# The first loads of a gated cross-attention and mixture-of-experts kernel on two DMA queues, with idle matmuls ahead of the first real one

## The chip, the cores and the metric

The kernel runs on one core of one Trainium2 chip. The metric is the device time of that core in microseconds (us), lower is better. The kernel before takes 236.41 us, the median of 3 runs (236.2 to 236.48).

## What is computed

Cut to what matters, for x of 8 x 256 x 256 and a context of 8 x 120 x 256 (float32):

```
q = layernorm(x) @ Wq + bq;  k = ctx @ Wk + bk;  v = ctx @ Wv + bv
x = x + tanh(g_xattn) * softmax(q @ k.T) * 256**-0.5 @ v      # per batch item
h = layernorm(x)
e = argmax(h @ router_w.T)                                    # one of 8 experts
x = x + tanh(g_ffn) * (silu(h @ gate_w[e].T) * (h @ up_w[e].T)) @ down_w[e].T
```

## The kernel before, in words

The kernel is written by hand, engine by engine, with semaphores. Each engine works through its own list in order, so an instruction that waits holds back all that stands behind it on that engine. The rows of x are 2,048 tokens, held as 16 tiles of 128 in `xin`, two tiles for each of the 8 batch items.

**First stage, around which the change lies.** The queries and keys are never built. One 256 x 256 matrix `MT` is made from the query and key weights, and its product with the context is `A`, so that the scores are the normalised x times `A`.

- SP issues the loads of `wkT` (L299), `wqT` (L300), the context `ctx_sb` (L301, in the buffer `both`), then the eight pieces of x (L306) with `wv` (L305) ahead of the third piece, then the first raw expert weights (L313, L324, L326).
- ACT issues, on its own DMA queue, the two gates (L517, L518: 4 bytes copied to each of 128 partitions), the value bias `bvb` (L519) and the router weights `wrT` (L520). It then waits for both gates (`d_g`, L521) and takes their tanh (L522). Only then does it come to the eviction of `MT` (L527 to L531), in two halves `m`, each behind TensorE's `t_mt`.
- TensorE waits for both weights (`d_wq`, L690), makes `MT` in PSUM (L693), then a small product with the bias (L699). It waits for the context (L703) and for both evicted halves of `MT` (`a_mt`, L704), makes `A` in four parts (L708), waits for `bvb` and `wrT` (`d_sm`, L713), runs L715, and then, once ACT has evicted `A` (L579), turns the normalised x of item 0 (L724), makes its values (L733) and its scores (L744).
- DVE subtracts on the weights (L951, L953), then takes the statistics of x items 0 and 1 as they land (L958, L962), their scales (L944 to L948) and their normalisation (L939). It waits for the tanh (L968) and for `d_sm` (L970), takes the statistics of the other six items (L958, L962), waits for TensorE's L715 (L972) and L733 (L979), and comes to `minima(0)` (L985), which needs the scores of item 0. Behind that stand the scales of the other items and the normalisation of item 2.
- POOL makes constants (L358 to L378).

**Attention loop.** For each of the 8 items the engines pass a tile round: TensorE transposes and multiplies, ACT takes exponentials, DVE minima, residuals and statistics. ACT also splits the first three experts' weights into high and low parts between items (`split_first`, L583), and POOL makes the low parts (L409, L413) as soon as ACT's high part is there.

**Routing and experts.** Tokens are sorted by expert, then up to 23 tiles of 128 tokens are gathered, multiplied with their expert's weights (L876, L888) and scattered. Before each of two waits in the routing, TensorE runs useless bf16 matmuls (`spin`, L822).

The lines in question:

```
pe.wait_ge(d_wq, 32)                       # L690, then L693, L699
pe.wait_ge(d_ctx, 16)                      # L703
pe.wait_ge(a_mt, C)                        # L704, then L708
act.wait_ge(d_g, 32)                       # L521
act.activation(tg[:], gates[:], ACT.Tanh)  # L522, then L526: act.wait_ge(t_mt, m + 1)
```

Of the kernel before, what the change touches and what calls it, by code (L numbers as in the profile page):

```python
# [26 lines left out]
BF16 = mybir.dt.bfloat16  # L27
# [6 lines left out]
P = 128  # L34
B, S, H = 8, 256, 256
# [3 lines left out]
C = H // P  # L39
# [21 lines left out]
def flamingo_moe(nc, x, ctxT, g_x, g_f, WqT, WkT, Wv, bv, WrT, Wgu, Wd, WdL, out):  # L61
    with ExitStack() as stack:
        def sb(name, shape, dt=F32):
            return stack.enter_context(nc.sbuf_tensor(name, shape, dt))

        def sem(name):
            return stack.enter_context(nc.semaphore(name))
# [7 lines left out]
        ctx_sb = both[:, 0:C * B * K].rearrange("p (c n) -> p c n", c=C)  # L75
# [5 lines left out]
        wqT = sb("wqT", [P, C, H + 1])  # L81
# [37 lines left out]
        x1 = sb("x1", [P, 2, TB, H])  # L119
# [2 lines left out]
        rs2 = sb("rs2", [P, 2, NTOK])  # L122
        x1T = wkT[:, :, 0:H]
        wqx = xnT
        pick = sb("pick", [P, NTOK])
        oh = sb("oh", [P, NTOK + 1, E], BF16)

# [15 lines left out]
        def part(room, start, *dims):  # L143

            size = 1
            for d in dims:
                size *= d
            names = " ".join("abc"[:len(dims)])
            view = room[:, start:start + size]
            if len(dims) > 1:  # L150
                view = view.rearrange(f"p ({names}) -> p {names}", **dict(zip("abc", dims)))
            return view, start + size
# [3 lines left out]
        ohlo, _ = part(free_c[:, at:at + NTOK * P // 2].bitcast(BF16), 0, NTOK, P)  # L156
        at += NTOK * P // 2
        uv, _ = part(free_c[:, at:at + NTOK * NT].bitcast(BF16), 0, NTOK, 2, NT)

        rsel, _ = part(V[:].rearrange("p b h -> p (b h)")[:, 0:NTOK * 3 * NT].bitcast(BF16), 0, NTOK, 6, NT)  # L160
# [3 lines left out]
        idx8, _ = part(free_m[:, at:at + NTOK * 8].bitcast(U32), 0, NTOK, 8)  # L164
# [20 lines left out]
        ps = stack.enter_context(nc.psum_tensor("ps", [P, 8, 512], F32))  # L185
# [3 lines left out]
        d_wv, d_wq, d_ctx, d_sm, d_g = sem("d_wv"), sem("d_wq"), sem("d_ctx"), sem("d_sm"), sem("d_g")  # L189
# [7 lines left out]
        t_v, v_v = sem("t_v"), sem("v_v")  # L197
        t_a, a_a = sem("t_a"), sem("a_a")
        v_wqx, t_wqbk = sem("v_wqx"), sem("t_wqbk")
        v_chain = sem("v_chain")  # L200
        v_st1 = sem("v_st1")
        v_xn, t_t1, a_xnT = sem("v_xn"), sem("t_t1"), sem("a_xnT")
        t_s, v_max, a_exp = sem("t_s"), sem("v_max"), sem("a_exp")
# [78 lines left out]
        def newton_fused(eng, chain, mean, rs, nm, n):  # L282

            ve, y, a = nwt[:, 0, 0:n], nwt[:, 1, 0:n], nwt[:, 2, 0:n]
            for step in range(3):
                chain(eng.tensor_tensor(a, y, y, ALU.mult))
                chain(eng.scalar_tensor_tensor(out=a, in0=a, scalar=-0.5, in1=ve, op0=ALU.mult, op1=ALU.mult))
                chain(eng.scalar_tensor_tensor(out=rs if step == 2 else y, in0=a, scalar=1.5, in1=y, op0=ALU.add, op1=ALU.mult))
            return eng.scalar_tensor_tensor(out=nm, in0=mean, scalar=-1.0, in1=rs, op0=ALU.mult, op1=ALU.mult)
# [4 lines left out]
        @block.sync  # L294
        def _(sp):
            def ap(t, c):
                return t.rearrange("(c p) n -> p c n", c=c)

            sp.dma_start(wkT[:], ap(WkT, C)).then_inc(d_wq, 16)  # L299
            sp.dma_start(wqT[:], ap(WqT, C)).then_inc(d_wq, 16)  # L300
            sp.dma_start(ctx_sb, ap(ctxT, C)).then_inc(d_ctx, 16)  # L301
            xv = x.rearrange("b (t p) h -> b p t h", p=P)
            for b in range(B):
                if b == 2:
                    sp.dma_start(wv[:], ap(Wv, C)).then_inc(d_wv, 16)  # L305
                sp.dma_start(xin[:, TB * b:TB * b + TB, :], xv[b]).then_inc(d_x[b], 16)  # L306

            def load_gu(e):
                if e >= RAW:

                    sp.wait_ge(a_hg, e - RAW + 1)
                    sp.wait_ge(p_lg, e - RAW + 1)
                sp.dma_start(raw_gu[:, e % RAW], Wgu[e]).then_inc(d_gu[e], 16)  # L313

            def load_d(e):
                if e == SPLIT + 1:

                    sp.wait_ge(t_stat, 1)
                elif e:

                    sp.wait_ge(a_hd, e if e <= SPLIT else e - 1)
                    sp.wait_ge(p_ld, e if e <= SPLIT else e - 1)
                place = raw_d[:, 1 if e <= SPLIT else e % 2]
                sp.dma_start(place[:, 0:CI - 1].rearrange("p c n -> p (c n)"), Wd[e]).then_inc(d_d[e], 16)  # L324
                for start in (0, LAST):
                    sp.dma_start(place[start:start + LAST, CI - 1, :], WdL[e]).then_inc(d_d[e], 16)  # L326

            def arrived_gu(e):
                sp.wait_ge(d_gu[e], 16)  # L330
                sp.sem_inc(gu_ready, 1)

            def arrived_d(e):
                sp.wait_ge(d_d[e], 48)
                sp.sem_inc(d_ready, 1)  # L335

            load_gu(0)
            load_d(0)
            load_gu(1)
            for e in range(SPLIT + 1):  # L340
                arrived_gu(e)
                if e:
                    load_d(e)
                arrived_d(e)
                if e < SPLIT:
                    load_gu(e + RAW)
            for e in range(SPLIT + 1, E):
                if e >= SPLIT + RAW:
                    load_gu(e)
                load_d(e)  # L350
                arrived_gu(e)
                arrived_d(e)
# [161 lines left out]
        @block.scalar  # L514
        def _(act):
            rv = rows[0:N].rearrange("(b t p) h -> b p t h", p=P, t=TB)
            act.dma_start(gates[:, 0:1], g_x.to_broadcast([P, 1])).then_inc(d_g, 16)  # L517
            act.dma_start(gates[:, 1:2], g_f.to_broadcast([P, 1])).then_inc(d_g, 16)  # L518
            act.dma_start(bvb[:], bv.to_broadcast([P, H])).then_inc(d_sm, 16)  # L519
# [56 lines left out]
            for q in range(4):  # L576
                n, m = q // 2, q % 2
# [109 lines left out]

        @block.tensor
        def _(pe):
            pe.wait_ge(d_wq, 32)  # L690
            for m in range(C):
                for c in range(C):
                    last = pe.matmul(ps[:, 4 + m, 0:H + 1], wkT[:, c, P * m:P * m + P], wqT[:, c, :],  # L693
                                     start=(c == 0), stop=(c == C - 1))
                last.then_inc(t_mt, 1)
            pe.wait_ge(v_wqx, 2)
            for m in range(C):
                for c in range(C):
                    last = pe.matmul(ps[:, 6, m:m + 1], wqx[:, c, P * m:P * m + P], wkT[:, c, H:H + 1],  # L699
                                     start=(c == 0), stop=(c == C - 1))  # L700
# [4 lines left out]
            for q in range(4):  # L705
                n, m = q // 2, q % 2
                for c in range(C):
                    last = pe.matmul(ps[:, q, 0:480], MT[:, c, P * m:P * m + P], ctx_sb[:, c, 480 * n:480 * n + 480],  # L708
                                     start=(c == 0), stop=(c == C - 1))
# [120 lines left out]
            for t in range(NTOK):  # L830
                last = pe.matmul(ps[:, 2, 0:2 * NT], ohlo[:, t, :], uv[:, t].rearrange("p a n -> p (a n)"),
                                 start=(t == 0), stop=(t == NTOK - 1))
# [88 lines left out]
        def _(dve):  # L921
# [22 lines left out]
            def scales(t):  # L944
# [2 lines left out]
                link(guess(dve, link, mv1[:, t, 1], n))  # L947
                newton_fused(dve, link, mv1[:, t, 0], rs1[:, t], nm1[:, t], n).then_inc(v_st1, 1)  # L948

            dve.wait_ge(d_wq, 32)  # L950
            dve.tensor_tensor(wqx[:, :, 0:H - 1], wqT[:, :, 0:H - 1], wqT[:, :, H - 1:H].to_broadcast([P, C, H - 1]),  # L951
                              ALU.subtract).then_inc(v_wqx, 1)
# [239 lines left out]
```

## Time and profile before

| what | us |
|---|---|
| median of 3 runs | 236.41 |
| the profiled execution, device time | 236.55 |
| its span, first to last instruction | 234.7 |
| TensorE busy | 201.2 (86% of the span) |
| DVE, ACT, POOL busy | 131.6, 107.7, 138.0 |

A profile is one execution, recorded by the hardware. Times within it are counted from the start of the span. A DMA issue appears on the queue of the engine that issued it (SPq, ACTq), and the time to landing runs from the start of the issue to the semaphore.
### The profile page before, as it was taken

The numbers are of one execution on the slowest core, as the hardware profiler recorded it, in microseconds if no ns is written. First come the engines' busy times: TensorE is split into PE (matmuls) and PEld (weight loads), VectorE is DVE, ScalarE is ACT, GpSimd is POOL, SyncE is SP. The second block draws the span as 40 slices with busy tenths as digits, with TensorE's granted clock in tenths as the row PEclk, the third lists the DMA queues.
The fourth block names the chain that finished last, engine by engine and source line by source line (L and its number), as shares of the span: only waits on it lengthen the run. The fifth ranks groups of instructions, "written<-read, shape, count | busy, mean of one in ns | idle before, by whom it ended". The sixth has DMA issues, their size and how long they took to land.

```text
span 234.7 us, 4522 instructions
## 1 busy us (share of the span) xinstructions
PE 201.2 (86%) x1211; PEld 173.1 (74%) x1211; DVE 131.6 (56%) x426; ACT 107.7 (46%) x217; POOL 138.0 (59%) x135
## 2 busy tenths in 40 slices
PE   0797799997674878999999999999999999999640
PEld 0645688895573857888888888888888888888520
DVE  0389689975769302555553745564637555656410
ACT  2234567766430043368348565459485224443200
POOL 3000009779169789436984998987989973331110
PEclk9999999999979578999999999999999999999955
DMA  4999211774900022951093066094002021110000
GB/s 86 367 382 382 94 47 56 242 263 132 362 27 0 13 80 69 355 182 44 13 357 107 22 216 251 19 353 135 1 27 66 4 71 42 49 49 1 9 25 14
DMA packets 11826, 29.42 MB, mean 125 GB/s; under 512 B 2223, under 2 KB 8242, under 8 KB 10771
## 3 DMA queue, kind: packets, MB, share of 16 engines
q1 hardware_dynamic: 6848, 21.70, 26.1%
q0 software_dynamic: 2064, 5.12, 7.1%
q10 hardware_dynamic: 2882, 2.24, 2.8%
q8 instruction: 14, 0.23, 0.4%
q14 instruction: 18, 0.14, 0.2%
HBM read 24.85 MB, written 4.72 MB: 126 GB/s over the span
## 4 chain that ended last, share of the span: by engine, by line
PE 63%; POOL 10%; DVE 8%; DMA 8%; issue 4%; ACT 3%; SPq 1%; ACTq 0%; POOLq 0%; DVEq 0%
PE ps L876 33%; PE ps L888 12%; PE ps L855 6%; PE ps L891 5%; DMA xin<-in_x 4%; POOL wgu L409 3%; DMA both<-in_WdL 3%; DVE st L958 2%; PE ps L848 2%; PE ps L762 2%; POOL wd L413 2%; DMA xin<-x_rows,table 1%; ACT wgu L564 1%; POOL both L442 1%; ACT prob L547 1%
## 5 line engine op out<-in xcount | busy, mean ns | idle before, releaser
L876 PE MATMUL ps<-wgu,xhT 128*128 x360 | 83.0, 384 | 1.2 <-DVE xhT L1106 1.2
L876 PEld LDWEIGHTS ps<-wgu,xhT 128*128 128x128 f32 x360 | 66.2, 191 | 12.4 <-issue 1.4
L888 PE MATMUL ps<-wd,hT 128*128 x120 | 43.7, 400 | 2.1 <-DVE hT L1115 2.1
L386 POOL TENSOR_TENSOR wgu<-raw_gu,wgu (+1 forms) x12 | 38.6, 3247 | 0.1
L468 POOL DMA_INDIRECT xin<-x_rows,table x23 | 22.6, 982 | 26.4 <-DVE xin L1136 21.6
L1123 DVE TENSOR_TENSOR A<-xin,ps 128x512 f32<-128x512 f32 (+1 forms) x40 | 20.6, 520 | 25.4 <-ACT xin L640 14.6
L409 POOL TENSOR_TENSOR wgu<-raw_gu,wgu 128x352 fp32r<-128x352 f32 x16 | 14.5, 945 | 34.5 <-ACT wgu L564 34.5
L640 ACT ACTIVATE xin<-ps 128x512 f32<-128x512 f32 (+1 forms) x40 | 18.6, 465 | 31.4 <-PE ps L876 31.3
L473 POOL DMA_INDIRECT out<-xin,table x20 | 20.3, 1016 | 20.7 <-DVE xin L1136 15.5
L891 PE MATMUL ps<-wd,hT 128*128 x100 | 28.4, 284 | 0.0
L888 PEld LDWEIGHTS ps<-wd,hT 128*128 128x128 f32 x120 | 22.9, 191 | 6.6 <-issue 2.3
L634 ACT ACTIVATE hT<-ps 128x512 fp32r<-128x512 f32 x20 | 11.8, 592 | 32.9 <-PE ps L855 32.9
L1133 DVE SCALAR_TENSOR_TENSOR xin<-ps,tg,xin 128x256 f32<-128x256 f32 x20 | 9.7, 483 | 24.8 <-PE ps L888 24.8
L1111 DVE TENSOR_TENSOR hT<-ps,hT 128x512 fp32r<-128x512 f32 x20 | 13.8, 692 | 14.8 <-ACT hT L634 14.2
L564 ACT ACTIVATE wgu<-raw_gu (+1 forms) x16 | 21.5, 1376 | 0.0
L390 POOL TENSOR_TENSOR wd<-both,wd (+1 forms) x6 | 21.1, 3512 | 0.0
L621 ACT ACTIVATE A<-xin,stat 128x256 f32<-128x256 f32 x22 | 13.4, 607 | 16.0 <-DMA xin<-x_rows,table 16.0
L891 PEld LDWEIGHTS ps<-wd,hT 128*128 128x128 f32 x100 | 19.2, 192 | 0.0
L855 PE MATMUL ps<-ident,A 128*128 128x128 f32 x120 | 16.4, 273 | 0.7 <-DVE A L1125 0.7
L855 PEld LDWEIGHTS ps<-ident,A 128*128 128x128 f32 x120 | 14.2, 140 | 2.5 <-DVE A L1125 1.0
L564 ACT ACTIVATE wd<-both (+1 forms) x8 | 11.8, 1475 | 2.2 <-SPq L335 2.2
L1106 DVE TENSOR_TENSOR xhT<-ps,xhT 128x256 fp32r<-128x256 f32 x21 | 8.9, 424 | 6.2 <-ACT xhT L627 5.6
(149 smaller groups left out, 296.2 us busy)
## 6 DMA issues: line engine op xcount, KB each, us to landing
raw_gu<-in_Wgu SPq DMA_DIRECT2D x8, 1408.0 KB, 6.4
both<-in_Wd SPq DMA_DIRECT2D x8, 640.0 KB, 4.2
xin<-in_x SPq DMA_DIRECT2D x8, 256.0 KB, 8.0
x_rows<-x ACTq DMA_DIRECT2D x8, 256.0 KB, 3.0
both<-in_WdL SPq DMA_DIRECT2D x16, 64.0 KB, 4.6
both<-in_ctxT SPq DMA_DIRECT2D x1, 960.0 KB, 8.0
xin<-x_rows,table POOLq DMA_INDIRECT x23, 3.6
out<-xin,table POOLq DMA_INDIRECT x20, 2.6
```

What stands on the lines that cost most here:

```text
L386: ins = pool.tensor_tensor(lo, src, hi, ALU.subtract)
L390: pool.tensor_tensor(wd[:, slot, :, 1, :].rearrange("p o c n -> p (o c) n"), raw_d[:, raw].rearrange("p r c n -> p (r c) n"), wd[:, slot, ...
L409: ins = pool.tensor_tensor(wgu[:, e, 1, c, n], src, wgu[:, e, 0, c, n].bitcast(F32), ALU.subtract)
L468: pool.indirect_dma_start(out=xg[:, j % SEATS, :], out_offset=None, in_=rows, in_offset=bass.IndirectOffsetOnAxis(ap=table[:, j:j + 1], ax ...
L473: pool.indirect_dma_start(out=out, out_offset=bass.IndirectOffsetOnAxis(ap=table[:, j:j + 1], axis=0), in_=og[:, j % RING, :], in_offset=N ...
L564: return act.activation(dst, src, ACT.Copy)
L640: act.activation(halves(sg, half), gate(half), ACT.Silu).then_inc(a_sg, 1)
L855: last = pe.transpose(ps[:, 4 + c // 4, P * (c % 4):P * (c % 4) + P], hm[:, P * c:P * c + P], ident[:])
L876: last = pe.matmul(ps[:, g, 0:2 * WIDE if g < 2 else 4 * REST], xhT[:, j % 2, x_part, c, :], w, start=(c == 0 and (x_part, w_part) == (0, 0)),
L888: last = pe.matmul(ps[:, 6, 0:2 * H], hT[:, 0, c, :], wd[:, slot, c].rearrange("p o a n -> p (o a n)"), start=(c == 0), stop=(c == CI - 1) ...
L891: pe.matmul(ps[:, 6, 0:H], hT[:, 1, c, :], wd[:, slot, c, 0, :].rearrange("p o n -> p (o n)"), start=False, stop=False, skip_group_check=True)
L1123: ins = dve.tensor_tensor(halves(hm, half), halves(sg, half), up_of(half), ALU.mult)
```

## The change

The query weights and the context are no longer loaded by SP behind the key weights. ACT issues them on its queue, ahead of the gates, the bias and the router weights. On SP's queue x follows the key weights directly. DVE first sets a bf16 view of 128 x 512 (`quiet`, in the room of `x1`, free at that time) to 1.0, and TensorE waits for it and runs nine matmuls on it, each 512 columns wide, into PSUM bank 7, ahead of its wait for the weights. Nothing reads their result.

```diff
+        quiet = x1[:, 0, 0, :].bitcast(BF16)
...
             sp.dma_start(wkT[:], ap(WkT, C)).then_inc(d_wq, 16)
-            sp.dma_start(wqT[:], ap(WqT, C)).then_inc(d_wq, 16)
-            sp.dma_start(ctx_sb, ap(ctxT, C)).then_inc(d_ctx, 16)
...
             rv = rows[0:N].rearrange("(b t p) h -> b p t h", p=P, t=TB)
+            act.dma_start(wqT[:], WqT.rearrange("(c p) n -> p c n", c=C)).then_inc(d_wq, 16)
+            act.dma_start(ctx_sb, ctxT.rearrange("(c p) n -> p c n", c=C)).then_inc(d_ctx, 16)
             act.dma_start(gates[:, 0:1], g_x.to_broadcast([P, 1])).then_inc(d_g, 16)
...
         def _(pe):
+            pe.wait_ge(v_quiet, 1)
+            for _ in range(9):
+                pe.matmul(ps[:, 7, 0:2 * H], quiet[:, 0:P], quiet[:], start=True, stop=True)
             pe.wait_ge(d_wq, 32)
...
+            dve.memset(quiet, 1.0).then_inc(v_quiet, 1)
             dve.wait_ge(d_wq, 32)
```

## Rows read from the trace of the kernel before

**Rows 1.** The page of before: its first line

```profile
span 234.7 us, 4522 instructions
```

**Rows 2.** Chain of waits in order of time, 0 to 62: start us, length us, what

```profile
2.30 8.33 DMA xin<-in_x
...
34.62 7.38 POOL wgu L409 x8
```

**Rows 3.** Timeline of DVE: start us, us, engine, line, what, count, [idle before <-releaser]

```profile
10.65 1.51 DVE L958 BATCH_NORM_STATS2 st<-xin 128x6 f32<-128x256 f32 x4 [2.83 <-DMA xin<-in_x]
...
16.67 0.35 DVE L971 TENSOR_SCALAR bvb<-bvb,tgn 128x256 f32<-128x256 f32 x1
...
22.61 0.40 DVE L985 TENSOR_REDUCE negmax<-ps 128x2 f32<-128x240 f32 x1
```

**Rows 4.** Timeline of ACT and PE, same columns as rows 3

```profile
6.79 0.20 ACT L522 ACTIVATE tg<-gates 128x2 f32<-128x2 f32 x1 [2.68 <-DMA gates<-in_g_f]
...
7.07 3.79 PE L693 MATMUL ps<-wqT,wkT 128*128 128x257 f32 x8 [7.07 <-DMA wqT<-in_WqT]
...
10.65 1.38 PE L699 MATMUL ps<-wkT,xnT 128*128 128x1 f32 x8
10.90 0.17 ACT L527 ACTIVATE negc<-ps 128x1 f32<-128x1 f32 x1 [1.04 <-PE ps L693]
...
11.10 0.47 ACT L530 ACTIVATE MT<-ps,negc 128x255 f32<-128x255 f32 x1
...
11.89 6.69 PE L708 MATMUL ps<-both,MT 128*128 128x480 f32 x16
...
20.69 1.14 PE L744 MATMUL ps<-A,xnT 128*128 128x120 f32 x8
```

**Rows 5.** DMA issues by tile: count, KB each, us from issue to landing

```profile
both<-in_ctxT SPq DMA_DIRECT2D x1, 960.0 KB, 8.0
...
wkT<-in_WkT SPq DMA_DIRECT2D x1, 257.0 KB, 4.4
wqT<-in_WqT SPq DMA_DIRECT2D x1, 257.0 KB, 5.7
...
bvb<-in_bv ACTq DMA_DIRECT2D x1, 128.0 KB, 7.2
...
gates<-in_g_f ACTq DMA_DIRECT2D x1, 0.5 KB, 5.5
wrT<-in_WrT ACTq DMA_DIRECT2D x1, 8.0 KB, 8.1
```

**Rows 6.** Timeline of the queues of SP and ACT, same columns as rows 3

```profile
0.79 0.44 SPq L299 DMA_DIRECT2D wkT<-in_WkT  x1
...
1.80 0.46 SPq L301 DMA_DIRECT2D both<-in_ctxT  x1
1.80 0.48 ACTq L519 DMA_DIRECT2D bvb<-in_bv  x1
...
2.31 0.48 ACTq L520 DMA_DIRECT2D wrT<-in_WrT  x1
```

**Rows 7.** Stretches of 4 us: busy by engine, then PEclk, DMA share, GB/s

```profile
2.00:6.00 4.00, 0.00 (x0) 0.00 (x0) 0.00 (x0) 1.28 (x1) 0.95 (x7) 1.00 0.58 128
6.00:10.00 4.00, 2.93 (x7) 2.38 (x8) 0.77 (x2) 0.88 (x4) 0.00 (x0) 1.00 1.04 380
```

**Rows 8.** Matmuls of two lines: ns min/median/max, first and last start

```profile
L693 PE MATMUL ps<-wqT,wkT x8: 635/635/793, 7.1 to 10.2; 128*128 128x257 f32 x8
...
L708 PE MATMUL ps<-both,MT x16: 566/566/649, 11.9 to 18.0; 128*128 128x480 f32 x16
```

**Rows 9.** Stretches around a gap of TensorE, same columns as rows 7

```profile
64.80:66.20 1.40, 0.11 (x1) 0.02 (x1) 1.26 (x9) 0.41 (x2) 0.93 (x4) 0.98 0.18 61
66.40:69.20 2.80, 2.80 (x36) 2.80 (x35) 1.36 (x8) 1.13 (x1) 2.06 (x10) 0.50 0.03 9
69.60:71.60 2.00, 2.00 (x39) 2.00 (x37) 1.71 (x10) 0.00 (x0) 1.64 (x8) 1.00 0.00 0
```

More of the change, by code:

```diff
@@ L199, in flamingo_moe @@
         v_wqx, t_wqbk = sem("v_wqx"), sem("t_wqbk")
-        v_chain = sem("v_chain")
+        v_chain, v_quiet = sem("v_chain"), sem("v_quiet")
         v_st1 = sem("v_st1")
```

## The prediction, made before the changed kernel was run

> **What bounds the kernel now.** I began with the page's first line, which gives the span [rows 1]. The profiled execution took 236.55 us, 0.14 above the median of 236.41, so I add a change of the path to the median. Then the chain of waits in order of time, its first 62 us, because the diff touches only the first microseconds. It starts with the landing of x at 10.63 and, through DVE, TensorE and ACT, reaches POOL's low parts of the expert weights at 34.62, which start when ACT has made the high part inside the attention loop [rows 2]. From there to the end it is relay work, so whatever moves the start of that loop moves the end by about as much.
>
> The timeline of DVE shows why x bounds. DVE starts its statistics when x lands (10.65), has no wait of note, and reaches `minima(0)` (L985) at 22.61 [rows 3]. The timeline of TensorE shows the rival branch. The weights land at 7.07, L693 and L699 run, ACT evicts the second half of `MT` from 10.90 to 11.57, `A` (L708) starts at 11.89, and the scores of item 0 end at 20.69 + 1.14 = 21.83 [rows 4]. `minima(0)` needs both, so the reader is to see that the TensorE branch has 22.61 - 21.83 = 0.78 us of slack and no more. Any gain above 0.78 us must come from both branches.
>
> **The loads.** Landings are issue plus time to landing [rows 5, 6]: `wkT` 0.79 + 4.4 = 5.2, `wqT` 7.07, the second gate 6.8, `bvb` 1.80 + 7.2 = 9.0, context 1.80 + 8.0 = 9.8, `wrT` 2.31 + 8.1 = 10.4, x 10.65 [rows 3, 4]. From 2 to 6 the DMA engines moved about 127 GB/s, from 6 to 10 about 380 [rows 7]. The first stretch is 0.51 MB, just the two weights. The second fits the order of the issues: bvb and context are 1.11 MB, 2.9 us at 0.38 MB/us, data complete at 8.9 and landed 0.9 later.
>
> Both queues share those engines, and the landings alternate between them: the second gate just ahead of `wqT`, `bvb` ahead of the context, `wrT` ahead of x. Within each queue they came in order of issue, so I put a gate that is issued behind the context behind it. The Trainium skill ("DMA: Bandwidth & Descriptors", Queues, rings and completion order) says that each DMA engine takes the descriptors of one ring in order and goes round robin between rings by packet. The landings here agree with it, down to the alternation.
>
> **What the change does to them.** On SP's queue: `wkT`, x0, x1, `wv`, x2 and so on. On ACT's: `wqT`, context, gate, gate, `bvb`, `wrT`. ACT's own issues grow from four to six, some 0.5 us each [rows 6], so it is through at about 3.8 instead of 2.8, before any data it needs: that costs nothing. The nine matmuls and the memset run before any weight can be there: nothing either.
> - x0 moves ahead of the context. 0.98 MB less in front is 2.6 us at most; with the context's packet in between, less. DVE starts 0.5 to 3 us earlier, and I take 1.5.
> - The context lands with x0 in front: 0.26 MB, 0.7 us later than now, less the `bvb` (0.13 MB, 0.3 us), and less what the first stretch gives back.
> - **The gates go last, and ACT waits for them before it evicts `MT`** (L521). The late bound: the first stretch still ends at 6.0, then x0, context, x1 and `wv` pass (1.77 MB, 4.6 us), landing 1.0 later: 11.6. The early bound: the weights take half of their 4 us because the gates are gone from beside them, done at 4.0; x0 and context 3.3, x1 0.7, and both gates 0.7 (two gates have as many small rows as `wrT`, which landed 1.4 after `bvb` with an x piece of 0.7 beside it), landing 1.0 later: 9.7. Nothing decides between them, so I take the middle, 10.7. Now it is 6.8, and it has been harmless.
> - Then on ACT, one after the other: tanh 0.20, and twice 10.90 to 11.57 = 0.67 for the halves of `MT`, with a hop of 0.03, then 0.3 to L708 [rows 4]: 10.7 + 1.9 = 12.6, against 11.89 now. L708 to the end of the scores is 9.94 us [rows 4], so with the clock at full speed the scores end at 22.5. That spends all of the slack: `minima(0)` stands at about 22.6, as before. Between the bounds: -0.95 (scores at 21.6) to +0.95 us.
>
> **The clock.** L693 starts its eight records 0.44 us apart for 257 columns, L708 its sixteen 0.41 us apart for 480 [rows 8], so the first ran at the lower level (1.2 GHz) and the second at the upper (2.4 GHz), although the profile shows a granted clock of 1.00 in both, presumably having no record of it yet. The nine matmuls are 512 columns each, about 0.43 us at the lower level, from about 1.3 to 5. If they raise the clock, L693 saves half of 8 x 0.44 = 1.8 us. But that saving ends in front of L704, which now waits for the gates: with the weights at 5 to 7 TensorE is through L699 at about 8 to 9.5 and idles until 12.6, 3 to 4.5 us. The trace shows what such a gap does: with 0.11 us busy in 1.40 the granted clock was 0.98, in the next 2.8 us, all busy, it was 0.50, and only then 1.00 [rows 9]. Before, L693 and L699 ran right up to L708 and it started at full speed. I take one such stretch, cut a little since the work after it is denser: 2 us of L708 at half speed costs 1.0 us. The bounds are 0 (no fall) and 1.8 (3.6 us at half speed, as long as L693 took, 7.07 to 10.65 [rows 4]).
>
> The Trainium skill ("TensorE: Matmul & The Clock Gate", HAM oscillation) warns that waits for DMA between bursts throttle the clock again each time. By it the gap ahead of L708 undoes the warm-up, and rows 9 agree for a gap elsewhere in the kernel. Without such a fall the sum would be 0.0 instead of +1.0.
>
> **Sum.** Gates and MT: 0.0. Clock: +1.0. All else is hidden. DVE arrives at about 21.1 and waits. 236.41 + 1.0 = 237.4 us. A measurement of this kernel can tell about 0.2%, 0.47 us, from no change.
>
> **The rivals.**
> - *The TensorE branch keeps its clock and the gates come at the middle time.* Against it stand rows 9, for it that the gap may be short if the weights land late. The time is 236.4 to 236.6.
> - *Faster: the gates land early and the clock holds.* The place is L521. If they land by 10.2 the scores end by 22.0, below the time at which DVE reaches `minima(0)` now, and DVE with its earlier x profits. At the early bound 9.7, -0.95 us: 235.5. If ACT's queue gets the engines nearly alone, gates at 9 give -1.6: 234.8. For it: the slow first stretch has room, engines busy only 0.58 of it. Against: the gates' rows are themselves the likeliest reason for it, and they are only moved.
> - *Slower by more*: gates at 11.6 and a full stretch at the lower level: 0.95 + 1.8 gives 239.2. `d_sm` could also be late for DVE at L970, needed at 16.67 less 1.5 [rows 3], but `bvb` and `wrT` follow the gates by 1 to 2 us, so at 13.6 they are in time.
> - *The warm-up does not warm.* Then L693 stays at half speed, and with late gates even this is hidden; L708 may start slow as well. It is the forecast's time.
>
> **Chances.** Slower through late gates, the clock or both, 0.52, of which the forecast's own size is most; no measurable change, where early gates and a fallen clock or middle gates and a full clock cancel, 0.21; faster 0.27, since the landing times are bounds and not rows. Four times in ten I give the clock no fall. The range goes from 235.3, just beyond the early gates with the full clock, to 239.2, both bounds on the slow side.
>
> **What would show it.** Right: tanh (L522) at about 10.9 instead of 6.79, with an idle time released by the gates; L708 at 12.6 or later; its records 0.8 us apart at first; L693's eight records 0.21 us apart and done before the gates land; DVE idle ahead of L985, released by TensorE. Wrong: tanh before 9.5, or L708 before 11.9 at 0.41 us a record. Then the chain would run through DVE and come out shorter. A weight landing near 5 says that the gates had held the first stretch up.

## The result and the profile after

The changed kernel takes 238.81 us, the median of 20 runs (238.19 to 241.72), against 237.07 for the kernel before, measured over 20 runs (235.77 to 239.81). The ratio is 1.0078, 95% interval 1.0054 to 1.0102: 0.8% slower, 1.8 us. The forecast was slower by 1.0. Below, a median is over all executions of a kernel, while a ratio with its interval leaves out those more than 1.5% above the fastest of the same kernel, so the two can differ.

The profiled execution took 239.01 us with a span of 236.9. Its chain of waits in order of time (start, length, what) no longer runs through the landing of x but through that of the second gate:

```profile
2.36 8.53 DMA gates<-in_g_f
...
12.39 9.12 PE ps L712 x16
...
24.79 0.41 DVE negmax L990
...
36.81 7.37 POOL wgu L408 x8
```

The chain runs from the gates through ACT's eviction of `MT` and the whole of `A` to `minima(0)` at 24.79, where the one of before had 22.61 [rows 3]. POOL's low parts start at 36.81 instead of 34.62 [rows 2]: 2.18 us at `minima(0)` are 2.19 us there. The timeline of DVE (start, length, engine, line, what, idle before and its releaser):

```profile
6.37 0.75 DVE L963 BATCH_NORM_STATS2 st<-xin 128x6 f32<-128x256 f32 x2 [1.18 <-DMA xin<-in_x]
...
9.71 0.75 DVE L963 BATCH_NORM_STATS2 st<-xin 128x6 f32<-128x256 f32 x2 [2.59 <-DMA xin<-in_x]
...
14.97 0.35 DVE L976 TENSOR_SCALAR bvb<-bvb,tgn 128x256 f32<-128x256 f32 x1
...
24.79 0.41 DVE L990 TENSOR_REDUCE negmax<-ps 128x2 f32<-128x240 f32 x1 [0.49 <-PE ps L748]
```

x0 is there at 6.37, x1 not until 9.71, and the long wait is now at the end, for TensorE. The timeline of ACT and TensorE, same columns:

```profile
1.51 4.02 PE L693 MATMUL ps<-x 128*128 128x512 bf16 x9 [1.51 <-DVE x L954]
...
5.32 2.76 PE L697 MATMUL ps<-wqT,wkT 128*128 128x257 f32 x8
...
7.92 0.95 PE L703 MATMUL ps<-wkT,xnT 128*128 128x1 f32 x8
...
10.91 0.20 ACT L523 ACTIVATE tg<-gates 128x2 f32<-128x2 f32 x1 [5.69 <-DMA gates<-in_g_f]
...
11.78 0.47 ACT L531 ACTIVATE MT<-ps,negc 128x255 f32<-128x255 f32 x1
...
12.39 9.11 PE L712 MATMUL ps<-both,MT 128*128 128x480 f32 x16 [3.53 <-ACT MT L531]
...
23.61 1.14 PE L748 MATMUL ps<-A,xnT 128*128 128x120 f32 x8
```

The tanh stands at 10.91 (6.79 before), idle 5.69 us for the gate; `MT` (L531) is through at 12.25, `A` (L712) starts at 12.39 after 3.53 us of idle TensorE, and takes 9.11 us where it took 6.69 [rows 4]. The DMA issues (KB, us to landing) and three stretches (last columns granted clock, DMA share, GB/s):

```profile
both<-in_ctxT ACTq DMA_DIRECT2D x1, 960.0 KB, 6.7
...
wkT<-in_WkT SPq DMA_DIRECT2D x1, 257.0 KB, 3.1
wqT<-in_WqT ACTq DMA_DIRECT2D x1, 257.0 KB, 3.6
...
gates<-in_g_f ACTq DMA_DIRECT2D x1, 0.5 KB, 8.5
```

```profile
2.00:6.00 4.00, 4.00 (x11) 1.89 (x10) 0.77 (x2) 1.28 (x1) 0.95 (x7) 1.00 1.02 345
6.00:10.00 4.00, 2.87 (x15) 2.39 (x14) 1.04 (x3) 0.00 (x0) 0.00 (x0) 1.00 0.61 199
8.00:9.00 1.00, 0.87 (x9) 0.78 (x7) 0.00 (x0) 0.00 (x0) 0.00 (x0) 1.00 0.25 53
```

The weights landed at 3.9 and 4.4, the context at 1.33 + 6.7 = 8.0 (before 9.8), the second gate at 2.36 + 8.5 = 10.9. The slow stretch of [rows 7] has not gone, it has moved: 345 GB/s from 2 to 6, then 53 GB/s from 8 to 9. The stretches of the gap and of `A`:

```profile
8.90:12.30 3.40, 0.00 (x0) 0.00 (x0) 2.29 (x13) 1.39 (x8) 0.00 (x0) 0.73 0.85 271
12.40:17.00 4.60, 4.60 (x6) 2.15 (x7) 4.32 (x17) 0.66 (x1) 0.00 (x0) 0.50 1.11 393
17.40:22.00 4.60, 4.45 (x15) 2.23 (x13) 2.92 (x20) 1.78 (x3) 0.00 (x0) 1.00 1.03 382
```

In the gap TensorE did nothing for 3.4 us, and the mean granted clock over it is 0.73: it is 1.00 up to 10.4 and 0.50 from 10.6, so it fell 1.6 us after TensorE had stopped. The first 4.6 us of `A` ran at 0.50, the rest at 1.00.

The spans differ by 236.9 - 234.7 = 2.2 us, but the shift does not simply ride through. The chain in order of time has these expert tiles:

```profile
87.64 4.12 PE ps L880 x18
...
93.78 3.83 PE ps L880 x18
...
120.47 5.24 PE ps L880 x18
...
175.46 5.15 PE ps L880 x18
```

The second tile starts at 93.78, only 0.24 us after the one of before (93.54 in its chain), largely because the first ran at the upper level here (granted clock 1.00 from 87.6 to 91.7) and took 4.12 us, where it had taken 5.66 (0.50 from 87 to 90). The sixth and one more then took 5.2 us instead of 3.83, at a granted clock of 1.00. So in this pair of profiles the 2.2 us at POOL are down to 0.24 at the second tile, and what separates the ends came later. Such swings of 1 to 2 us come and go between executions (the runs of before alone spread over 4 us), so one profile is read here up to POOL's start, and the medians say what reaches the end.

### The profile page after: what moved, and what is told of

Read it like the earlier page. It is cut to its first block, busy times and chain, and to the rows that moved or that the text cites. A ratio compares the mean times of both kernels' runs of the same rounds, so it can differ in the third digit from the quotient of the medians.

```text
span 236.9 us, 4541 instructions
## 1 busy us (share of the span) xinstructions
PE 205.5 (87%) x1220; PEld 173.3 (73%) x1220; DVE 132.0 (56%) x427; ACT 106.9 (45%) x217; POOL 138.0 (58%) x135
## 4 chain that ended last, share of the span: by engine, by line
PE 67%; DVE 9%; DMA 6%; POOL 5%; issue 4%; ACT 4%; ACTq 1%; SPq 0%; POOLq 0%; DVEq 0%
PE ps L880 32%; PE ps L892 11%; PE ps L859 5%; PE ps L895 5%; PE ps L712 4%; DMA gates<-in_g_f 4%; POOL wgu L408 3%; DMA both<-in_WdL 3%; PE ps L829 2%; PE ps L852 2%; PE ps L766 2%; POOL wd L412 2%; ACT wgu L565 1%; DVE V L1088 1%; DVE both L1079 1%
## 5 line engine op out<-in xcount | busy, mean ns | idle before, releaser
L880 PE MATMUL ps<-wgu,xhT 128*128 x360 | 81.5, 379 | 1.2 <-DVE xhT L1111 1.2
L880 PEld LDWEIGHTS ps<-wgu,xhT 128*128 128x128 f32 x360 | 65.2, 188 | 11.8 <-issue 1.4
L712 PE MATMUL ps<-both,MT 128*128 128x480 f32 x16 | 9.1, 736 | 3.5 <-ACT MT L531 3.5
```

The costliest lines, as they stand in the source:

```text
L880: last = pe.matmul(ps[:, g, 0:2 * WIDE if g < 2 else 4 * REST], xhT[:, j % 2, x_part, c, :], w, start=(c == 0 and (x_part, w_part) == (0, 0)),
```

## The experiments

Every ratio is to the kernel before on the same chip. `e1` to `e4` shared one chip, `e5` to `e8` a second, `before_again`, `e9`, `e10` and `e11` a third. Intervals are 95%. Ratios of different chips are compared only through that of before. The record names no chip for the changed kernel's own comparison. Where median and ratio part by more than 0.3% the text says so.

### Is it the gates?

`e1_tanh_late`, the changed kernel with the wait and the tanh moved down the ACT list:

```diff
-            act.wait_ge(d_g, 32)
-            act.activation(tg[:], gates[:], ACT.Tanh).then_inc(a_tg, 1)
...
             act.activation(wqbk[:], ps[:, 6, 0:C], ACT.Copy, scale=-1.0).then_inc(a_wqbk, 1)
+            act.wait_ge(d_g, 32)
+            act.activation(tg[:], gates[:], ACT.Tanh).then_inc(a_tg, 1)
```

> The changed kernel, with ACT's wait for the gates and the tanh moved behind the eviction of MT and of the bias product. Theory (the gates hold MT and so L712): MT is evicted when TensorE has made it, by about 8.6; A starts at about 9, as soon as L703 is through and the context has landed (8.0), at full clock; the scores of item 0 end at about 19 instead of 24.75, DVE becomes the bound of minima(0) at about 20.9, 3.9 us earlier than in the changed kernel and 1.7 earlier than before: about 235.3 against 237.1. Rival (the context, or the clock by itself, holds L712): A starts no earlier than 11 and the time stays within 1 us of the changed kernel.

Measured: 236.45 against 236.65, ratio 0.9945 (0.9911 to 0.9978). The timeline of ACT, TensorE and DVE:

```profile
9.15 6.68 PE L712 MATMUL ps<-both,MT 128*128 128x480 f32 x16
...
11.11 0.21 ACT L534 ACTIVATE tg<-gates 128x2 f32<-128x2 f32 x1 [1.82 <-DMA gates<-in_g_f]
...
17.94 1.14 PE L748 MATMUL ps<-A,xnT 128*128 128x120 f32 x8
...
21.25 0.40 DVE L990 TENSOR_REDUCE negmax<-ps 128x2 f32<-128x240 f32 x1
```

`A` starts at 9.15 with the gates landing as late as ever, so the rival falls. `minima(0)` is at 21.25, and nothing but one wait and its tanh was moved. By the ratios the place of that wait costs 1.3% (1.0078 against 0.9945); the medians, 236.45 against 236.65, put e1 level with before and the cost at 0.8%, and POOL's start, 34.68 against 36.81, at 2.1 us or 0.9%. So it costs about 1%, and that e1 is faster than before is not sure. Of the 1.7 us promised against before, the ratio has 1.3 and the medians 0.2.

### Is it also the clock?

`e2_gap_filled`, the changed kernel with the gap ahead of `A` filled:

```diff
             last.then_inc(t_wqbk, 1)
+            for _ in range(14):
+                pe.matmul(ps[:, 7, 0:2 * H], quiet[:, 0:P], quiet[:], start=True, stop=True)
```

> The changed kernel with 14 more of the same bf16 matmuls behind L703, 14 x 0.216 = 3.0 us at the upper level, in the gap ahead of A. Theory (the clock fell in the gap and cost what the slow start of A shows): A starts at 12.4 as before the edit, but its sixteen records take 6.6 us instead of 9.1; minima(0) moves from 24.79 to 22.6 and the kernel comes out 2.2 us faster than the changed one, about level with the kernel before. Rival (the late start alone makes the loss, the clock does not matter): A takes 9.1 us again, the time stays.

Measured: 237.41, ratio 1.0017 (0.9981 to 1.0052). The timeline and the stretch:

```profile
12.42 6.68 PE L714 MATMUL ps<-both,MT 128*128 128x480 f32 x16 [0.60 <-ACT MT L531]
...
22.38 0.41 DVE L992 TENSOR_REDUCE negmax<-ps 128x2 f32<-128x240 f32 x1 [0.49 <-PE ps L750]
```

```profile
12.40:19.00 6.60, 6.58 (x18) 3.20 (x18) 6.29 (x24) 1.99 (x3) 0.00 (x0) 1.00 1.06 394
```

`A` starts at 12.42 as late as in the changed kernel, but at full clock, in 6.68 us. `minima(0)` moves by 2.41 us to 22.38, and POOL starts at 34.41, 2.4 us earlier too. The ratio holds 1 and its interval ends just below that of the changed kernel (1.0052 against 1.0054), so most of the loss is gone. So at this size the late start of `A` alone costs nothing that can be measured: it uses up TensorE's slack, as forecast. What makes the kernel slower is the clock that fell while TensorE waited for the gates. The profiled execution, 239.50 us, is one of the longest of e2, and its second expert tile starts at 93.83, no earlier than in the changed kernel: the gain at POOL is traced, its arrival at the end is not.

### The warm-up alone, and its absence

`e3_no_warm` is the changed kernel without the nine matmuls and the memset; `e4_warm_only` is the kernel before with them and nothing else.

```diff
-            pe.wait_ge(v_quiet, 1)
-            for _ in range(9):
-                pe.matmul(ps[:, 7, 0:2 * H], quiet[:, 0:P], quiet[:], start=True, stop=True)
...
-            dve.memset(quiet, 1.0).then_inc(v_quiet, 1)
```

> The changed kernel without the nine matmuls and the memset, loads as changed. Theory (the warm-up saves time only ahead of the wait for the gates): L697 runs at the lower level throughout and ends by 8.2, L703 by 9.6, still ahead of MT at 12.3; A starts at 12.4 and the time is that of the changed kernel within 0.5 us; if TensorE's later work keeps the clock up into A, it is even faster by up to 2 us. Rival (the warm-up is worth its 1 to 2 us): slower than the changed kernel by 1 us or more.

Measured: 239.42, ratio 1.0100 (1.0051 to 1.0149) from 6 runs, level with the changed kernel's 1.0078 within the intervals. The timeline:

```profile
4.73 3.79 PE L694 MATMUL ps<-wqT,wkT 128*128 128x257 f32 x8 [4.73 <-DMA wqT<-in_WqT]
...
12.76 8.18 PE L709 MATMUL ps<-both,MT 128*128 128x480 f32 x16 [3.17 <-ACT MT L531]
...
24.22 0.41 DVE L986 TENSOR_REDUCE negmax<-ps 128x2 f32<-128x240 f32 x1 [0.49 <-PE ps L745]
```

The product of the weights runs slowly, 3.79 us, and it does not matter: `A` waits for the gates again. `A` took 8.18 us, so the clock had fallen in this gap too (3.17 us).

> The kernel before with the nine matmuls and the memset alone, loads as before. Theory (DVE with x bounds minima(0), TensorE has slack): L693 runs in 1.8 us, A starts at about 10 instead of 11.9, the scores end by 20, minima(0) stays at 22.6 and the time stays within 0.5 us of before. Rival (the warm-up helps by itself): 1 us or more faster than before.

Measured: 238.18, ratio 1.0057 (1.0023 to 1.0091). That is neither: the warm-up alone makes the kernel before slower by 0.6%. The timeline and the stretches:

```profile
7.00 3.23 PE L697 MATMUL ps<-wqT,wkT 128*128 128x257 f32 x8 [2.06 <-DMA wqT<-in_WqT]
...
11.59 8.09 PE L712 MATMUL ps<-both,MT 128*128 128x480 f32 x16
...
22.97 0.41 DVE L990 TENSOR_REDUCE negmax<-ps 128x2 f32<-128x240 f32 x1 [0.36 <-PE ps L748]
```

```profile
4.94:7.00 2.06, 0.00 (x1) 0.00 (x1) 0.02 (x1) 0.20 (x1) 0.00 (x0) 1.00 0.76 258
9.00:11.50 2.50, 2.50 (x11) 2.23 (x10) 0.91 (x3) 0.92 (x4) 0.00 (x0) 0.50 1.10 358
...
15.00:19.00 4.00, 4.00 (x11) 1.90 (x10) 3.89 (x14) 1.95 (x3) 0.00 (x0) 1.00 1.05 420
```

Nine matmuls end at 4.94, 2.06 us before the weights land. They took 3.43 us instead of the 4.02 of the changed kernel, so the last of them ran at the upper level. The granted clock is still 1.00 when the gap ends; it falls at 7.6, 0.6 us into the product of the weights, is 0.50 from 9.0 to 11.5 with TensorE busy throughout, and `A` took 8.09 us. `minima(0)` came 0.36 us late in this execution, which is less than the 1.3 us of the ratio. But the profiled execution, 235.25 us, is the fastest of the 12 and itself faster than the median of before, so it can't show where the rest of the loss arises; I have not followed it.

`e11_long_warm` has 18 matmuls in place of e4's 9 (`range(9)` becomes `range(18)`) and leaves no such gap.

> e4_warm_only (loads as before) with 18 matmuls instead of 9, which fill TensorE up to the landing of the weights at 7. Theory (in e4 the gap of 2.06 us ahead of the weights let the clock fall during the work that followed, so A took 8.09 us): now L697 runs in 1.8 to 2 us, A at the upper level throughout in 6.7 us, minima(0) at 22.6 as before, since DVE bounds it; the time is within 0.5 us of before. Rival: A still takes 8 us, and the time is 1 us or more over before, as with e4.

Measured: 235.26 against 235.02, ratio 0.9995 (0.9948 to 1.0043). `A` starts at 10.70 and takes 6.68 us, `minima(0)` stands at 22.50. Without the gap `A` runs at full speed. The interval overlaps that of e4 (from 1.0023), so that the long warm-up does less harm than the short one is likely, not shown. It brings nothing: DVE bounds `minima(0)`, and TensorE, early, then stands idle for 2.72 us ahead of the item loop; from 23.1 to 28 the granted clock is 0.65 in the mean, and POOL starts at 34.92, no earlier than before.

### Where the gates stand, and what they cost

`e5_gates_last` is e1 with both gate loads behind the bias and the router weights; `e6_gates_first` is the changed kernel with them ahead of the query weights; `e7_no_gate_loads` has none, and two POOL memsets write the gates' values, which leaves that load out of the computation.

```diff
-            act.dma_start(gates[:, 0:1], g_x.to_broadcast([P, 1])).then_inc(d_g, 16)
-            act.dma_start(gates[:, 1:2], g_f.to_broadcast([P, 1])).then_inc(d_g, 16)
# and, in e7, on POOL ahead of its constants
+            pool.memset(gates[:, 0:1], 1.0).then_inc(d_g, 16)
+            pool.memset(gates[:, 1:2], -1.7600164413452148).then_inc(d_g, 16)
```

> e1_tanh_late with the two gate loads also moved to the end of ACT's queue, behind the bias and the router weights. Theory (while the gates are read, everything behind them on either queue waits, and they come between x0 and x1): x1 lands by 7.5 instead of 10.05, DVE comes to minima(0) at about 20 instead of 21.25, TensorE's gap ahead of the item loop shrinks with it, and the kernel is 1 to 1.5 us faster than e1, about 0.99 of before. Rival (x1 was late because of the context and the bandwidth): x1 stays at about 10 and the time that of e1.

> The changed kernel with the gate loads first on ACT's queue, ahead of the query weights; weights, context and x stay split over the two queues, the warm-up stays. Theory (the gates cost some 3 to 4 us of the engines' time wherever they stand): the query weights land at 7 to 8 instead of 4.4, the tanh is back at about 7, A starts at about 11, minima(0) at about 21.5, faster than the changed kernel by 2 us or more and than before by about 1. Rival (splitting the loads is what costs): no faster than the changed kernel.

> The changed kernel with no load of the gates: POOL writes their two values into the tile by memset, before anything else. Theory (the gates alone hold the tanh and take the engines): tanh at about 5.3, x1 by 7.2, the stretch from 6 to 10 moves over 340 GB/s instead of 199, A starts at about 8.9 when L703 is through, minima(0) at 20 or earlier; 3 us or more faster than the changed kernel. Rival: the first 10 us are slow for another reason, and the stretch stays under 250 GB/s.

Measured: e5 236.30, ratio 0.9962 (0.9925 to 0.9999); e6 237.07, 0.9986 (0.9923 to 1.0049); e7 236.28, 0.9952 (0.9911 to 0.9992). The landings of x1, by the second row of DVE's statistics, with the gates last and with no gates at all:

```profile
9.73 0.75 DVE L963 BATCH_NORM_STATS2 st<-xin 128x6 f32<-128x256 f32 x2 [2.44 <-DMA xin<-in_x]
...
20.93 0.40 DVE L990 TENSOR_REDUCE negmax<-ps 128x2 f32<-128x240 f32 x1
```

```profile
8.39 6.71 PE L712 MATMUL ps<-both,MT 128*128 128x480 f32 x16 [0.23 <-DMA both<-in_ctxT]
...
9.73 0.75 DVE L963 BATCH_NORM_STATS2 st<-xin 128x6 f32<-128x256 f32 x2 [2.53 <-DMA xin<-in_x]
...
20.92 0.40 DVE L990 TENSOR_REDUCE negmax<-ps 128x2 f32<-128x240 f32 x1
```

Half of each theory falls. x1 lands at 9.73 in both, as in the changed kernel, so the gates were not what delayed it; even with no gates the stretch from 8 to 9 moved 117 GB/s and that from 6 to 10 254, not the 340 expected. With the gates last, the stretches from 10 to 11 and 11 to 12, where they pass, moved 262 GB/s each, against 367 and 387 with no gates, so they cost far less there than in front (128 and 125 from 2 to 6). `A` at 8.39 in e7, after an idle 0.23 us for the context, says again that nothing but the gates had held it. In e6 the engines are slow from 2 to 6 once more, 125 GB/s, and the query weights land at 9.0, so there the gates do take the engines' time; `A` starts at 13.48, later than in the changed kernel, but at full clock (6.68 us), and `minima(0)` is at 23.45. That is 2 us later than I expected: the tanh is early again (7.42), but now the weights are late. e6 is level with before, and faster than the changed kernel by 0.9%, so splitting the loads is not what costs.

`e8_distinct_rows` keeps e7's memsets and puts in the gates' place two loads of as many 4-byte rows from 128 different addresses, whose data is not used:

```diff
+            act.dma_start(junk[:, 0:1], bv[0:1, 0:128].rearrange("o p -> p o")).then_inc(d_g, 16)
+            act.dma_start(junk[:, 1:2], bv[0:1, 128:256].rearrange("o p -> p o")).then_inc(d_g, 16)
```

> e7 with two loads of 128 rows of 4 bytes each in the gates' place, waited for in the same way, but from 128 different addresses (the value bias) instead of one address 128 times; their values are not used. Theory A (reading one address 128 times is what is slow): the stretch from 8 to 9 moves over 300 GB/s and the wait on ACT ends by 9.5. Theory B (rows of 4 bytes are slow wherever they come from): as in the changed kernel, 53 GB/s in that stretch and the tanh at about 10.9.

Measured: 237.85, ratio 1.0126 (1.0060 to 1.0192) from 8 runs. The DMA issue and the stretch from 8 to 9:

```profile
junk<-in_bv ACTq DMA_DIRECT2D x2, 0.5 KB, 7.3
```

```profile
8.00:9.00 1.00, 0.43 (x4) 0.35 (x4) 0.00 (x0) 0.00 (x0) 0.00 (x0) 1.00 0.79 174
```

Neither theory holds as put. With different addresses the loads took 7.3 us (median of the two) instead of the gates' 8.0 and 8.5 and the stretch moved 174 GB/s instead of 53. Over the wider stretch from 6 to 10 it is 258 GB/s, against 254 with no such loads (e7) and 199 with the gates, so what the gates take from the engines there goes with reading one address 128 times. The rows of 4 bytes are not free either: from 10 to 11 it is 235 against e7's 367, and the wait for them ends at 10.13, 1.7 us after the context. The kernel is no faster (its medians, 237.85 against 237.05, give 1.0034, so the size of the loss is unsure), because the table load of ACT (1.28 us) fell behind the new wait and the tanh came at 11.42, later than in the changed kernel.

### Where e1's gain went, and a version that keeps it

e1, e5 and e7 gained 1.4 to 1.7 us at `minima(0)`, but POOL's low parts started at 34.68, 35.09 and 35.09, no earlier than before (34.62). The stretches of e5 show it:

```profile
19.10:22.20 3.10, 0.00 (x0) 0.00 (x0) 2.89 (x23) 1.39 (x5) 0.00 (x0) 1.00 1.07 346
22.60:25.90 3.30, 2.78 (x14) 2.50 (x13) 2.76 (x12) 0.43 (x2) 0.00 (x0) 0.51 0.46 194
26.00:29.00 3.00, 3.00 (x8) 2.19 (x7) 0.00 (x0) 2.40 (x6) 0.00 (x0) 0.50 0.00 0
```

TensorE, early now, stands idle for 3.1 us until DVE brings `minima(0)`, and runs the first items at 0.50. Two edits test that. `e9_item_gap_filled` fills the gap of e5:

```diff
+            for _ in range(13):
+                pe.matmul(ps[:, 7, 0:2 * H], quiet[:, 0:P], quiet[:], start=True, stop=True)
             for i in range(B):
                 turn2(i)
```

> e5_gates_last with 13 more bf16 matmuls (2.8 us at the upper level) between turn1(1) and the first turn2, where e5 leaves TensorE idle for 3.15 us while DVE is the bound. Theory (what e1, e5 and e7 gained at minima(0) was given back because the clock fell in this gap): minima(0) stays at about 20.9, the item loop runs at the upper level from its start, POOL starts its low parts about 12.0 us after minima(0), as before, at 33 instead of 35.1, and the time is about 1.5 us less than e5's, 0.99 of before or less. Rival (the gain is lost elsewhere): POOL starts at 35 again.

`e10_no_warm_tanh_late` is e1 without warm-up and memset, so that TensorE is not early in the first place.

> e1_tanh_late without the nine matmuls and the memset. Theory (with the tanh out of the way DVE bounds minima(0) by 3 us, so the warm-up buys nothing, and its loss makes the gap in front of the item loop smaller): the product of the weights runs at the lower level from 4.7 to 8.3, A starts at 9.7, the scores end at about 20, minima(0) stays at 21.2 and the time is that of e1 or a little less. Rival (the warm-up pays once the tanh is moved): 1 us or more slower than e1.

Measured, against 235.02 on that chip: e9 233.20, ratio 0.9902 (0.9866 to 0.9938); e10 232.15, ratio 0.9880 (0.9814 to 0.9947), from 6 runs. The timeline and the stretches of e10:

```profile
4.33 3.79 PE L694 MATMUL ps<-wqT,wkT 128*128 128x257 f32 x8 [4.33 <-DMA wqT<-in_WqT]
...
9.49 8.46 PE L709 MATMUL ps<-both,MT 128*128 128x480 f32 x16
...
21.23 0.41 DVE L986 TENSOR_REDUCE negmax<-ps 128x2 f32<-128x240 f32 x1 [0.26 <-PE ps L745]
```

```profile
21.70:23.00 1.30, 0.00 (x0) 0.00 (x1) 1.06 (x8) 1.25 (x5) 0.00 (x0) 1.00 1.01 425
23.10:28.00 4.90, 4.20 (x29) 3.72 (x30) 3.17 (x13) 2.67 (x7) 0.00 (x0) 1.00 0.18 78
```

`A` takes 8.46 us, six records in the 3.3 us from 9.4 where e9 has ten, so without a warm-up it starts at the lower level. `minima(0)` is where e1 has it (21.25), the scores are only just ahead of it, TensorE's gap is 1.3 us instead of 3.0, and the clock stays at 1.00. POOL starts at 33.27, in e9 at 32.92, so the gain arrives, and the rival (the gain is lost elsewhere, POOL at 35 again) falls. Both beat the kernel before and, through it, the changed one: the split loads are worth 1.0 to 1.2% (e9 by its medians 0.8%) once the wait for the gates is out of the way and TensorE is neither late nor early. Between e9 and e10 the intervals do not decide.

Over all kernels the ratio follows POOL's start: where it is 1.6 to 2.2 us later than in the kernel before (the changed kernel, e3, e8) the ratios are 1.0078 to 1.0126, where it is 1.35 and 1.70 us earlier (e10, e9) 0.9880 and 0.9902, and in between 0.9945 to 1.0057. That is the evidence that a shift in the first stage reaches the end; from POOL's start to the first expert tile the single profiles differ by up to 4 us (49.5 in e4, 53.3 in e2).

### What a comparison can tell

> The kernel before, unchanged, as one of the compared kernels: its ratio to itself should have an interval that holds 1.000, and shows what a comparison of this length can tell. In its profile I look at the sixth expert tile, which took 3.83 us in the first profile of before and 5.1 to 5.3 in the profile of every other kernel so far. If it takes 5.2 here too, that tile has nothing to do with the edits; if 3.83, it does.

Measured: 235.13 against 235.02, ratio 1.0018 (0.9988 to 1.0048). The sixth expert tile took 3.83 us, as in e9, e10 and e11 on the same chip, while the changed kernel and `e1` to `e8` all show 5.1 to 5.3. `e9` contains all of e5's edits and `e11` is e4 with a longer warm-up, so that tile seems to go with the chip and not with the edits. The first profile of before has 3.83 as well, on a chip that is not on record, so this stays a guess, and the cause of the 5.2 us was not found. I leave it out of the account.

## Why the prediction was right

The direction, the range (235.3 to 239.2) and the likeliest mechanism came out; measured beside before, the loss is 1.8 us where I had 1.0. Of the 1.4 us between the forecast's 237.4 and the measured 238.81, 0.66 is the kernel before itself, whose median of 20 runs is 237.07 and not 236.41.

- **The bound.** That x, DVE and `minima(0)` set the end, with 0.78 us of slack for TensorE, held: e11 starts `A` 1.2 us earlier than before and gains nothing, e2 starts it 0.5 us later and loses nothing measurable. That a shift of `minima(0)` is passed on one to one held for the changed kernel as far as POOL (2.18 and 2.19), and the median moved by 1.8, though the profile itself does not show the shift arriving. For a gain it failed in the profiles of e1, e5 and e7, which lost theirs in the next gap. I had no term for that.
- **The gates.** Forecast landing 10.7, tanh 10.9, `A` at 12.6; measured 10.9, 10.91, 12.39. That they land behind the context held (8.0, then 10.9), and so did the order of issue within ACT's queue. The middle of the two bounds was right by luck of its parts: the weights came even before the early bound (landed at 4.4, not 5), and from the context's landing to the second gate's 2.9 us passed, where the early bound had 1.4 for x1 and the gates together. `A` started 0.2 us ahead of the 12.6 that I had named as the earliest sign.
- **The clock.** The mechanism held and the size did not: I took 1.0 us, with 1.8 as the outer bound, and `A` lost 9.11 - 6.69 = 2.42. The step at fault is "I take one such stretch, cut a little since the work after it is denser": `A` ran at 0.50 from its start at 12.39 to about 17.3, 4.9 us and not 2, and half of that is the 2.42. Worked through: `A` 0.50 later and 2.42 longer puts the scores 2.92 later (24.75 against 21.83), less the slack of 0.78 is 2.14, and `minima(0)` moved by 2.18. The forecast had 0.71 + 1.0 - 0.78 = 0.93.
- **x earlier.** 1.5 us taken, 1.7 measured (15.36 against 17.06 at the long statistics), and worth nothing, as forecast, since DVE then waited for the scores.
- **The warm-up.** It saves nothing in the changed kernel (e3), as forecast. It did not give the full speed either: the product of the weights (L697) took 2.76 us, between the 3.79 of the lower level and the 2.05 that e7 shows. That nine matmuls could do harm by themselves (e4) I had not foreseen.

That a wait between bursts brings the clock down was borne out for the gap of 3.5 us ahead of `A`, and for those of e1 (3.0 us) and e5 (3.1 us). The clock also fell after a gap of only 2.06 us in e4, which the Trainium skill ("TensorE: Matmul & The Clock Gate", HAM oscillation) does not lead one to expect. After gaps as short as that it went either way: it fell after 1.4 us in [rows 9] and held over 1.3 us in e10.

What stays open: why x1 lands at 9.7 even without the gates (the `bvb` load, one row of 1 KB read 128 times, is a suspect that was not tried; against it, in the kernel before it passed within the 380 GB/s of [rows 7]), and the part of e4's loss beyond 0.36 us.

## What to carry to other kernels

When loads are reordered, look for the smallest one and for the engine that waits for it: here 8 bytes, needed late, stood in an in-order list ahead of work that was needed early, and the wait belonged lower down. In these runs useless matmuls paid only where they reached almost up to the real work (e2, e9), and not always there (e11); a warm-up that ends early, or that makes TensorE early for its next wait, moves the slow stretch instead of removing it. Compare the work before a gap with what comes after it, since two branches that arrive together can keep the clock better than one that hurries, as e10 (a gap of 1.3 us, no fall) does beside e1 (3.0 us).

## What the hardware did that I had not expected

- Two loads of 128 rows of 4 bytes, all from one address, went with a microsecond in which all DMA traffic was down to 53 GB/s (117 without them, e7). Where they stood first (the kernel before and e6) the engines ran at 125 to 128 GB/s from 2 to 6; where they stood last (e5) it was 262 GB/s from 10 to 12.
- The clock fell to 0.50 not in a gap but within dense work: in e4 at 7.6, 0.6 us after the end of a gap of 2.06 us.
- The profile shows a granted clock of 1.00 from the start of the span, also where the pace of the matmuls is that of the lower level (the nine matmuls of 512 columns took 4.02 us, 0.43 each from start to start).
